# Packing the loads of a second scan, adding its residual rows a chunk later, and putting attention's sums ahead of its value copies

## The reference

```python
# first scan, over time, with a gate; h starts as cond_1024
gate = sigmoid(h @ Wh.T + z_t @ Wz.T + b)
h    = tanh(h * (1 - alpha) + gate * z_t)
# attention over its states: 16 heads of 8, relative keys and values
scores = (q . k  +  q . rel_k[q - k]) / sqrt(8)
attn   = softmax(scores)
out    = attn @ v + sum_k attn * rel_v[q - k]
x      = x + out @ Wo.T + bo
# second scan over the new x, h starts as cond_1024 again
h = tanh(x_t @ Wx + b2 + h @ Wh2)
# experts: the best 2 of 8 for each of 4096 rows
p = softmax(h @ router_w.T);  top 2, weights made to sum to 1
y = sum over the two of  weight * (gelu(h @ w1[e].T + b1[e]) @ w2[e].T + b2[e])
return x + y
```

## Time and profile before

| | |
|---|---|
| median of 3 runs | 721.68 us (721.23 to 728.16) |
| profiled execution, its time | 715.85 us |
| its span | 714.0 us |
| instructions | 27771 |
| TensorE matmul busy | 572.4 us (80%) |
| TensorE weight loads | 437.9 us (61%) |
| VectorE | 428.5 us (60%) |
| ScalarE | 394.0 us (55%) |
| GpSimd | 393.7 us (55%) |
| DMA | 108.48 MB, mean 152 GB/s |

### The profile page before, as it was taken

How to read it: one execution, slowest core, us unless ns; L and a number is a source line. 1 busy time by engine, 2 the same in 40 slices (tenths; PEclk the granted TensorE clock), 3 DMA queues, 4 the chain that set the end, 5 groups by cost and what they waited for, 6 DMA issues and landing times. The chain is left out here.

```text
span 714.0 us, 27771 instructions
## 1 busy us (share of the span) xinstructions
PE 572.4 (80%) x10475; PEld 437.9 (61%) x10475; DVE 428.5 (60%) x2008; ACT 394.0 (55%) x1113; POOL 393.7 (55%) x433
## 2 busy tenths in 40 slices
PE   2888888888777999899999967777733999999930
PEld 1556555555566677666766743333323999999930
DVE  1666666666555777787778530667681555555537
ACT  4666666666412555555555523344422999999920
POOL 4444555544424988888889611467772554545520
PEclk9999999999978999999999988699955999999975
DMA  7355656654594766666667206811121222222247
GB/s 256 120 208 207 222 195 224 219 208 179 216 282 122 204 186 184 193 192 189 183 195 208 91 2 189 269 41 56 51 81 49 68 67 73 67 67 73 65 135 240
DMA packets 115950, 108.48 MB, mean 152 GB/s; under 512 B 9232, under 2 KB 88592, under 8 KB 115584
## 3 DMA queue, kind: packets, MB, share of 16 engines
q1 hardware_dynamic: 109408, 95.18, 42.3%
q0 software_dynamic: 4320, 8.89, 3.8%
q10 hardware_dynamic: 2112, 2.89, 1.1%
HBM read 59.31 MB, written 45.52 MB: 147 GB/s over the span
## 5 line engine op out<-in xcount | busy, mean ns | idle before, releaser
L512 POOL TENSOR_TENSOR sc<-sc,mx 128x1024 f32<-128x1024 f32 x64 | 121.5, 1899 | 52.3 <-DVE mx L670 52.1
L406 POOL TENSOR_SCALAR QD<-q_all,mask 128x128 f32<-128x128 f32 x126 | 88.7, 717 | 98.5 <-DVE pre L361 95.4
L670 DVE CUSTOM_DVE_ANT_0 sc<-banks,s2t 128x128 f32<-128x128 f32 x512 | 113.0, 286 | 44.1 <-PE banks L563 44.0
L1142 POOL DMA_INDIRECT expert_outputs<-yr,xr x71 | 71.1, 1001 | 73.6 <-DVE yr L1313 67.7
L725 ACT ACTIVATE PT<-banks 128x512 f32<-128x512 f32 x128 | 69.9, 596 | 70.6 <-PE banks L576 70.6
L1085 ACT ACTIVATE hid<-banks,w1b 128x128 f32<-128x128 f32 x284 | 81.2, 369 | 14.2 <-PE banks L1021 14.2
L352 DVE COPY s2stage<-banks 128x512 f32<-128x512 f32 (+1 forms) x90 | 76.6, 852 | 16.5 <-PE banks L253 16.5
L1134 POOL DMA_INDIRECT expert_inputs<-rows,slotu x64 | 63.2, 988 | 40.0 <-DVE slotu L1244 22.6
L253 PE MATMUL banks<-RK,QD 32*128 32x128 f32 x1024 | 78.5, 454 | 3.9 <-DVE s2stage L352 0.9
L1021 PE MATMUL banks<-xt,w1b 128*128 128x128 f32 x568 | 76.7, 279 | 0.0
L1038 PE MATMUL banks<-w2b,hid 128*128 128x128 f32 x568 | 75.2, 275 | 0.3 <-ACT hid L1085 0.3
(11 more groups left out here) (132 smaller groups left out, 1020.3 us busy)
## 6 DMA issues: line engine op xcount, KB each, us to landing
s_scratch<-s2stage SPq DMA_DIRECT2D x32, 1024.0 KB, 4.8
s2t<-s_scratch SPq DMA_DIRECT2D x64, 512.0 KB, 4.4
xr<-expert_inputs SPq DMA_DIRECT2D x71, 64.5 KB
xz<-in_xz SPq DMA_DIRECT2D x8, 512.0 KB, 5.8
yb<-expert_outputs SPq DMA_DIRECT2D x16, 256.0 KB, 4.0
k_all<-in_xT SPq DMA_DIRECT2D x1, 2048.0 KB, 9.5
w1a<-in_w1T SPq DMA_DIRECT2D x1, 2048.0 KB
w2all<-in_w2T SPq DMA_DIRECT2D x1, 2048.0 KB
```

The costliest lines, as they stand in the source:

```text
L406: op = pool.tensor_scalar(QD[G % 3][:, :, h, :], q_all[:, :, quad(G)].rearrange("p b t -> p t b"), mask[:, h:h + 1], None, ALU.mult)
L512: pool.tensor_tensor(sc[U % RING][:], sc[U % RING][:], mx[U % RING][:].unsqueeze(2).broadcast_to([P, HH, T]), ALU.subtract)\
L670: op = dve.tensor_tensor_reduce(out=sc[r][:, h, :], in0=ps[2 * (U % 2) + h // 4][:, h % 4 * T:(h % 4 + 1) * T], in1=s2t[r][:, h, :], scale ...
L1142: pool.indirect_dma_start(yg_dram, bass.IndirectOffsetOnAxis(xr[k][:, D:].bitcast(U32), 0), yr[k][:], None).then_inc(s_ys[k], 16)
```

## The change

Three things.

1. In attention's slots VectorE makes the sums of unit `S + 3` before it copies the values of slot `S`, not after.
2. The constants of the router and the output bias are one array in DRAM, `packed` (128 x 471), already repeated over the partitions, and are loaded in one DMA. The residual rows are laid out so that each partition's 16 KB lie together; weights and biases of the experts are joined, again with rows already repeated. So four loads take the place of the twenty-two of before, and they wait on `s_rin` = 16 and `s_win` = 32. On the chip the constants are slices of one tile.
3. `add_rows(0)` moves from VectorE's step for `m = 0` to the end of its step for `m = 1`, just before `add_rows(1)`; with it the wait for `s_xrow`, now 16.

```diff
--- before.py
+++ after.py
@@ -696,12 +696,12 @@
                     for S in range(NU + 3):
-                        if S + 1 < VG // 2:
-                            copy_values(dve, VG // 2 + 1 + S, 7)
                         if S >= 4 and S % 2 == 0:
                             normalise_values((S - 4) // 2)
                         if S + LEAD < NU:
                             scores(S + LEAD)
+                        if S + 1 < VG // 2:
+                            copy_values(dve, VG // 2 + 1 + S, 7)
...
@@ -761,17 +761,13 @@
-        rwT = sb("rwT", [P, E])
-        bo_bc = sb("bo_bc", [P, D])
-        upper = sb("upper", [P, P])
+        widths = {"rwT": E, "upper": P, "iota": E, "ebase": E, "mult": MT, "tri": E * E, "tiles": NS, "padid": E + NULL,
+                  "destf": 2 * JT, "bo": D}
+        packed = sb("packed", [P, sum(widths.values())])
...
@@ -886,26 +882,14 @@
-                for dst, src in ((rwT[:], a["rwT"]), (upper[:], a["upper"]), 
-                                 (iota[:], a["iota"].partition_broadcast(P)),
...
-                                 (padid[:], a["padid"]), (destf[:], a["dest"])):
-                    sp.dma_start(dst, src).then_inc(s_rin, 16)
-                sp.dma_start(x1r[:], a["xrow"].rearrange("(n p) d -> p n d", p=P)).then_inc(s_xrow, 16)
-                sp.dma_start(bo_bc[:], a["bo"].partition_broadcast(P)).then_inc(s_xrow, 16)
-                sp.dma_start(w1a[:, :, 0:FF], a["w1T"]).then_inc(s_win, 16)
-                sp.dma_start(w1a[:, :, FF:], a["b1c"]).then_inc(s_win, 16)
-                sp.dma_start(w2all[:, :, 0:FC * D], a["w2T"].rearrange("p e f d -> p e (f d)")).then_inc(s_win, 16)
-                for e in range(E):
-                    sp.dma_start(w2all[:, e, FC * D:], a["b2"][e].partition_broadcast(P)).then_inc(s_win, 16)
-
+                sp.dma_start(packed[:], a["packed"]).then_inc(s_rin, 16)
+                sp.dma_start(x1r[:], a["xrow"]).then_inc(s_xrow, 16)
+                sp.dma_start(w1a[:], a["w1b1"]).then_inc(s_win, 16)
+                sp.dma_start(w2all[:], a["w2b2"]).then_inc(s_win, 16)
                 sp.wait_ge(s_pad, 1)
...
@@ -1191,8 +1175,6 @@
                 def step(m, scan_on, route_on):
                     if not route_on:
-                        dve.wait_ge(s_xrow, 32)
-                        add_rows(m)
                         return
...
@@ -1274,13 +1256,16 @@
+                    if m == 1:
+                        dve.wait_ge(s_xrow, 16)
+                        add_rows(0)
                     if scan_on:
                         add_rows(m)
                     dve.wait_ge(s_slot, c + 2)
```

More of the change, by code:

```diff
@@ L763, in build @@
         w2all = sb("w2all", [P, E, FC * D + D])
-        rwT = sb("rwT", [P, E])
-        bo_bc = sb("bo_bc", [P, D])
-        upper = sb("upper", [P, P])
-        ones = sb("ones", [P, P])
[L768 to L774, removed]
+        widths = {"rwT": E, "upper": P, "iota": E, "ebase": E, "mult": MT, "tri": E * E, "tiles": NS, "padid": E + NULL,
+                  "destf": 2 * JT, "bo": D}
+        packed = sb("packed", [P, sum(widths.values())])
+        rwT, upper, iota, ebase, mult, tri, tiles, padid, destf, bo_bc = (
+            packed[:, sum(list(widths.values())[:i]):sum(list(widths.values())[:i + 1])] for i in range(len(widths)))
+        tri = tri.rearrange("p (a b) -> p a b", b=E)
+        ones = sb("ones", [P, P])
         pad = sb("pad", [P, E + NULL, D + 1])
@@ L907, in _ @@
                 sp.wait_ge(s_null, 16)
-                sp.wait_ge(s_win, 16 * (3 + E))
+                sp.wait_ge(s_win, 32)
                 sp.wait_ge(s_end, 1)
@@ L1076, in _ @@
                 act.wait_ge(s_tab, TLINKS)
-                act.wait_ge(s_win, 16 * (3 + E))
+                act.wait_ge(s_win, 32)
                 act.sem_inc(s_hid, 2)
@@ L1120, in _ @@
             def _(pool):
-                pool.wait_ge(s_rin, 144)
+                pool.wait_ge(s_rin, 16)
                 pool.memset(ones[:], 1.0)
@@ L1151, in _ @@
                 dve.sem_inc(s_slot, 1)
-                dve.wait_ge(s_rin, 144)
+                dve.wait_ge(s_rin, 16)
                 dve.wait_ge(s_pad, 1)
@@ L1281, in _ @@
                 chunks(step)
-                dve.wait_ge(s_win, 16 * (3 + E))
+                dve.wait_ge(s_win, 32)
                 dve.sem_inc(s_xt, 2)
@@ L1345, with rows @@
     xt = f(x).transpose(2, 1, 0)
+    def rows(v):
+        return np.tile(np.asarray(v, np.float32)[None, :], (P, 1))
     arrays = {
         "xT": xt,
-        "xrow": f(x).transpose(1, 0, 2).reshape(T * B, D),
+        "xrow": f(x).transpose(1, 0, 2).reshape(NT, P, D).transpose(1, 0, 2),
         "wod": f(L0_attn_Wo),
-        "bo": f(L0_attn_bo),
         "xz": np.stack([np.zeros_like(xt), xt], axis=-1),
@@ L1362 @@
         "ident": np.eye(P, dtype=np.float32),
-        "w1T": f(L0_ffn_expert_w1).transpose(2, 0, 1),
-        "w2T": f(L0_ffn_expert_w2).reshape(E, D, FC, P).transpose(3, 0, 2, 1),
-        "b1c": f(L0_ffn_expert_b1).reshape(E, FC, P).transpose(2, 0, 1),
-        "b2": f(L0_ffn_expert_b2),
-        "rwT": f(L0_ffn_router_w).T,
-        "iota": np.arange(E, dtype=np.float32),
-        "upper": np.triu(np.ones((P, P), np.float32), 1),
-        "ebase": np.arange(E, dtype=np.float32) * CAP,
-        "mult": np.arange(MT, dtype=np.float32) * P,
-        "tri": np.tril(np.ones((E, E), np.float32)).ravel(),
-        "tiles": np.arange(NS, dtype=np.float32),
-        "padid": (2 * N + np.arange(E + NULL)[None, :] * P + np.arange(P)[:, None]).astype(np.float32),
-        "dest": (np.arange(2)[None, :, None] * N + np.arange(JT)[None, None, :]
-                 + np.arange(P)[:, None, None] * JT).reshape(P, 2 * JT).astype(np.float32),
+        "w1b1": np.concatenate([f(L0_ffn_expert_w1).transpose(2, 0, 1),
+                                f(L0_ffn_expert_b1).reshape(E, FC, P).transpose(2, 0, 1)], axis=2),
+        "w2b2": np.concatenate([f(L0_ffn_expert_w2).reshape(E, D, FC, P).transpose(3, 0, 2, 1).reshape(P, E, FC * D),
+                                rows(f(L0_ffn_expert_b2).ravel()).reshape(P, E, D)], axis=2),
+        "packed": np.concatenate([
+            f(L0_ffn_router_w).T, np.triu(np.ones((P, P), np.float32), 1), rows(np.arange(E)), rows(np.arange(E) * CAP),
+            rows(np.arange(MT) * P), rows(np.tril(np.ones((E, E))).ravel()), rows(np.arange(NS)),
+            2 * N + np.arange(E + NULL)[None, :] * P + np.arange(P)[:, None],
+            (np.arange(2)[None, :, None] * N + np.arange(JT)[None, None, :]
+             + np.arange(P)[:, None, None] * JT).reshape(P, 2 * JT),
+            rows(f(L0_attn_bo))], axis=1).astype(np.float32),
     }
```

6 lines of the change are left out of this document (1 added, 5 removed).

## The result

| | before | after |
|---|---|---|
| median of 20 runs | 719.71 us | 713.12 us |
| profiled execution, its time | 715.85 us | 711.60 us |
| its span | 714.0 us | 709.8 us |

The changed kernel is faster by 1.0%: ratio 0.9902, 95% interval 0.9877 to 0.9926, which is 7.1 us (5.3 to 8.9). The forecast was 717.0 us and 4.7 us less. Two executions of the changed kernel took 2482 us, with no profile and no cause known: the median of 713.12 counts them, the ratio leaves them and a third of 718.90 out, and the other seventeen have a median of 712.82, just under the forecast's range of 713 to 721.5. The median that stood ahead of the prediction, 721.68, was one of three runs; over twenty it is 719.71. So of the 3.9 us between 717.0 and 713.12 the first 2.0 are the level that I counted from. The rest is the sum.

What follows compares the result with a forecast made beforehand. It took the chain of waits, TensorE carrying most, as the bound, with VectorE hand-offs in attention and late instruction fetches in the second scan. Terms -3.8 - 1.9 + 1.0 = -4.7 us took 721.68 to 717.0 us, range 713 to 721.5.

Steps and rivals of the forecast that it cites:

- Sums ahead of copies: Attention's start: VectorE's sums no longer wait behind value copies, so TensorE's waits of 2.46 and 1.45 us go; -3.8 us.
- Rival B: Attention gives little because the clock falls in the rearranged stretch; 719.9 us, chance 0.15.
- Constants: Second scan: ten small loads become one, but TensorE first wants them at step 16 and enters without a stop; 0.
- Loads: Second scan: loads of whole rows end sooner, cutting TensorE's instruction-fetch stops from 4.84 to 2.9 us; -1.9 us.
- rival A: Second scan: no stops at all, since whole rows move quicker and are over sooner; 713.1 us, chance 0.15.
- Rows later: Second scan, step 32: TensorE's output products wait for VectorE's later addition to chunk 0's rows; +1.0 us.
- After the scan: GpSimd's scatter of chunk 6 moves with the scan one to one, null tiles unwaited for; 0.
- Rival C: Second scan, step 18: long rows make the instruction fetch wait for everything queued, stop 14.3 us; 728.4 us, chance 0.08.
- Rival D: Second scan: the stops are not fetches and stay, with the new wait beside them; 718.9 us, chance 0.12.

Runs made afterwards that it cites:

- e1_attn: Kernel before with only attention's order changed (sums ahead of value copies), old loads and rows: 714.65 us, ratio 0.9945.
- e3_rows: Kernel before with only the first rows' addition moved a chunk later, old loads and attention: 719.87 us, ratio 1.0018.
- e4_scan: Changed kernel with attention's order put back as before, keeping packed loads and later rows: 717.56 us, ratio 0.9953 to before.
- e2_loads: Kernel before with only the four packed loads, rows added at their old place, attention as before: 716.72 us, ratio 0.9971.
- g1_early: Changed kernel with add_rows(0) moved ahead of the slots of chunk 0, on a slower third chip: 772.45 us, ratio 0.9943 to before there.
- h1_steady: Changed kernel with each of the two weight loads made four times, two in flight at all times: 720.45 us, ratio 1.0002 to before there.
- h2_spread_early: Changed kernel with weights in eight pairs of pieces and first rows added ahead of chunk 0's slots: 710.24 us, ratio 0.9851 to before there.

## Why the prediction was wrong, and where it was right

1. *Sums ahead of copies, -3.8.* Right in mechanism and size. e1_attn gives 4.0 us (1.8 to 6.0). At the fourth content scores the profiles are 228.97 - 224.51 = 4.5 us apart, 0.7 more than forecast. Of that 0.15 is the earlier start (216.55) and 0.4 the shorter work up to them, in a stretch where the clock no longer falls. It reached the scan's block as 2.6, since this profile has the stop of the eighth group and that of before hasn't. Rival B expected the clock to fall in the rearranged stretch; it did the contrary.

2. *Constants, 0.* Nothing in the traces speaks against it. TensorE enters step 16 without a wait for them. GpSimd waits 12.0 us for the constants, and VectorE behind it 7.9 us for GpSimd's tiles, until 432.29; but then VectorE stands 8.85 us more for TensorE's logits, so the loop loses nothing.

3. *Loads, -1.9.* This is the step that failed. The mechanism holds: stops at 18 and 25, none at 32 and 38, the load over at about 446. The size doesn't. By the steps' excess it is -3.2 (5.78 to 2.54) and not -1.9. This is one pair of profiles: the four stops cost 4.4 to 6.1 us in the three with old loads (e1_attn, before, e3_rows), and step 25 alone 2.2 to 2.75 in the four with new ones on such chips, so the size is good to about a microsecond. What is the same in all seven is step 18: 1.18 to 1.51 with the old loads, no long step with the new. Most of the 1.3 between them is step 18, forecast to fall from 1.12 to 0.9, measured from 1.18 to nothing: 1.0. Its stop is 0.27 us and hidden in side work. I took 6.48 us for its fetch, the longest of three rows, though 5.65 and 6.20 stood beside it. TensorE entered step 11 at 433.72 and went on at 439.27:

```profile
433.72 0.33 PE L420 MATMUL banks<-h,wh 128*32 128x32 f32 x8
```

That is 5.55 us where the same stretch took 443.03 - 436.29 = 6.74 before. The instruction packet in it began 3.2 us after the entry (436.92) and not 4.1 (440.41 before). Why it began earlier isn't shown; the next one, also under the load of whole rows, took 4.4. Steps 32 and 38 were worth 1.08 and 1.27 where their rows say 0.71 and 1.04: 0.6, as a stop costs more than its row. Step 25, the other way, rose by 0.27 where I had 0.03. Beside the stops eight steps fewer are in the last column of the table, 0.5 us; the sum put the low clock at nothing and had it in rival A alone. The sums with the wait below: forecast -0.9, measured -2.9 in the profiles, -3.4 (-5.4 to -1.4) in e4_scan, which leaves -0.9 out. e2_loads, the loads alone, doesn't decide by its time: -2.1, anywhere from -4.5 to +0.2.

4. *Rows later, +1.0.* Right: 1.02 us of waiting, 0.86 of excess, at step 32, and not there as long as a stop covers it (e3_rows: 1.0018, with no change in its interval of 0.9997 to 1.004). That a stop at step 32 would hide it was the lower bound.

5. *After the scan, 0.* Off by 1.3 us: the 5.5 us by which the scan's last scatter came earlier arrived as 4.2.

*The level.* The sum stood on one profile and a median of three. The first was 3.9 us below the median of twenty and the second 2.0 above it. The difference was forecast too small by 1.9 us as the medians have it (2.4 by the ratio), and the level 2.0 too high, to the same side. The range of 713 to 721.5 had its lower end at rival A, no stops at all, which would have been 4.8 us; the result came to that edge by other ways, and that it came so near to rival A's 713.1 is chance: a stop of 2.25 us was still there. Rival C, the fetch that waits for everything in the queues, is out: the longest such stop of the scan in the kernels that load as the changed one does is 3.2 us (g1_early) and not 14. In the profiles of before and after, with the old mixture the instruction packets began 3.2 to 4.1 us after the entry, with whole rows 3.2 to 4.4, so longer rows made them little later. Rival D is out by h1_steady and h2_spread_early, whose stops come and go with the load.

The Trainium skill ("Runtime: NRT & Kernel Launch", Instruction fetch mechanics) has the sequencer fetching the next 16 KiB while it executes the present block. Seven stops one border apart and one packet of 16 KB between each two agree with that; that the fetch is hidden holds in h2_spread_early, not under full load.

## What to carry to other kernels

A bulk load beside a loop of short instructions on TensorE costs more than bandwidth: it delays the instructions. The packets of the instruction queue show that in a trace. Where it isn't urgent, ask for it in pieces, so that the DMA engines are half busy for long rather than full for a while; that gave another 3.5 to 4.4 us here. Before summing against a profile, see whether that execution lies within the timed ones, and use more than three of them: six profiles with the new attention differ by up to 7 us where the second scan starts. And when a stop is removed, look what it was hiding: here a wait of 1 us for an operation that only had to stand a few instructions earlier.

## What the runs showed of the hardware that I had not expected

- The distance from one instruction block to the next under full load is steady within one execution, 5.92 to 6.48 us in h1_steady. Over the executions it lay between 5.55 (step 11 to 18 after) and 7.02 (452.89 - 445.87 in e2_loads).
- At step 16 TensorE stops for 0.5 to 0.65 us in every trace, with the load (before) or without it (h2_spread_early, DMA share 0.07), so this one is not the load. What it is isn't shown. These are the two rows, from TensorE's weight loads:

```profile
440.00 0.15 PEld L420 LDWEIGHTS banks<-h,wh 128*32 128x32 f32 x5 [0.52 <-issue]
```

```profile
441.76 0.15 PEld L420 LDWEIGHTS banks<-h,wh 128*32 128x32 f32 x5 [0.52 <-issue]
```

- Two of four chips ran the kernel before 57 us slower and the changed one 60. In the trace of the changed one 53.5 us of it lie at the second scan's chunk starts, six times some 9 us, under waits that the profile can't name. A change in that stretch is worth measuring on more than one chip.
- The instruction stop in attention's eighth group, 1.8 to 4.5 us in eight of ten executions, at a DMA share of about 0.8 (242 to 249 us in the changed kernel), is larger than most effects of this study.
